# The last layer of a four-layer graph network: a gather per edge tile, or count matrices of block pairs applied by TensorE

## The chip, the cores and the metric

The kernel runs on one core of one Trainium2 chip. The metric is the device time of one execution in microseconds, lower is better. The engines are PE (TensorE, with its weight loads PEld), DVE (VectorE), ACT (ScalarE), POOL (GpSimd, which issues every indirect DMA here) and SP (SyncE, which issues plain DMAs).

## The reference

Four graph layers run one after the other over the same 3,125 nodes of 64 features and the same 103,125 directed edges (src, dst); after each, the result is added to x and normalised over its features. The last one is the one that the change rewrites:

```python
def _L3_gnn_ref(x, edge_index):
    from_, to_ = (edge_index[0], edge_index[1])
    n = x.shape[0]
    deg = jax.ops.segment_sum(jnp.ones_like(to_, dtype=x.dtype), to_, num_segments=n)
    deg_inv = jnp.where(deg > 0, 1.0 / jnp.sqrt(deg), 0.0)
    norm = deg_inv[from_] * deg_inv[to_]
    m_j = norm[:, None] * x[from_]
    out = jax.ops.segment_sum(m_j, to_, num_segments=n)
    return out
edge_index = jnp.stack([src, dst])
...
x = _layernorm(x + _L3_gnn_ref(x, edge_index), axis=-1)
```

Layer L0 is message passing with an edge network (4 inner layers), L1 an attention over edges with a tensor product, L2 message passing with edge features.

## The kernel before, in words

**Orders of the edges.** The nodes are cut into 25 blocks of 128. The edges are sorted twice by block, into 832 tiles of 128 edges each that never cross a block end: order "s" by src for L0, order "d" by dst for L1, L2 and L3. Sorting works in place numbers: DVE and PE compute for each edge its row in the sorted table (`ranks_s_*`, `totals_*`, `places_*`, L406 to L668), and POOL scatters the records there, one indirect DMA for each of 806 columns (`scatter_s_pool` L885, 8 bytes an edge; `scatter_d_pool` L899, 1,136 bytes an edge).

**Records stage.** While POOL scatters order "d", PE and ACT compute the two edge networks of L1 in 202 turns of four columns (`factor_pe` L994, `factor_act` L1030), and DVE copies the other fields of the record (`records_dve` L917). POOL's scatter of turn i waits for ACT's `eo` and DVE's `eo`; both wait until the scatter of turn i-4 has landed. All of it is written out, without loops.

**Messages stage**, four times for L0 and once for L2 (`edge_messages` L1123): 104 turns of 8 tiles. DVE copies 8 index columns (`gi`), POOL gathers 8 tiles of rows (L1161), PE multiplies with one-hot matrices, DVE adds each tile's sum to the block's column of `aggT`, whose number it has loaded into a register (`blocks_of` L1313).

**Attention stage** (`logits_*` L1758 to L1912): 208 turns of four tiles. POOL gathers 4 tiles in each (L1781) and waits for DVE's `gx_read` of four turns before (L1868). Then come the segment maximum by two scans (L1953 to L2060) and the weighted sums (`sums_*`, L2095 to L2155), 104 turns in which DVE adds each tile to its block.

**L3, the part that is rewritten** (from L2330). x times `dinv` is written to `xr` in DRAM; in 104 turns POOL gathers 8 tiles of rows (`conv_pool` L2350), DVE builds the one-hot matrix of the destinations for 8 tiles (L2387) and PE multiplies it with the gathered rows (L2372); DVE adds the 8 products to the blocks of `conv` (L2398), each at an offset from a register:

```python
for t, b in enumerate(blocks_of(dve, "d", i)):
    a = conv[:, bass.ds(b * D, D)]
    ins = dve.tensor_tensor(a, a, bank[j][:, t * D:(t + 1) * D], ALU.add)
```

Loops on an engine are built by `turns` (L105): some turns written out at both ends, the middle as a hardware loop of 2 or 4 turns. `join()` is a barrier of all engines, `meet()` one without POOL. Every engine runs its instructions in program order, and they meet by semaphores.

Of the kernel before, what the change touches and what calls it, by code (L numbers as in the profile page):

```python
# [5 lines left out]
ALU = mybir.AluOpType  # L6
# [59 lines left out]
assert MQ * KQ == TILES["d"] and KQ * H == P  # L66

# [54 lines left out]
def build(nc, x_in, src_in, dst_in, ea16, ea64, ea9, L0_W_in, L0_b_in, L0_eW1, L0_eb1, L0_eW2, L0_eb2, L0_nW1,  # L122
# [3 lines left out]
    with ExitStack() as ctx:  # L126
# [54 lines left out]
        xr2 = dram("xr2", [NPAD, XW])  # L181
        iota_done = sig("iota")
# [75 lines left out]
        bucket8 = tmp("bucket", [P, EC8])  # L258
        bucket = bucket8[:, 0:EC]
        member = tmp("member", [P, EC])  # L260
        onesw8 = tmp("onesw", [P, EC8])
        onesw = onesw8[:, 0:EC]
        rank8 = tmp("rank", [P, EC8])
        rank = rank8[:, 0:EC]
        pos8 = tmp("pos", [P, EC8])
        pos = pos8[:, 0:EC]
        ibuf = tmp("ibuf", [P, EC], I32)
# [17 lines left out]
        keyt = tmp("keyt", [P, 8 * P], BF16)  # L285
        EW = 4
# [664 lines left out]

        whole, left = TILES["s"] // P, TILES["s"] % P
# [41 lines left out]
        def factor_pe():  # L994
# [3 lines left out]
            def turn(k):  # L998
                if k.t == keys_at:
                    keys_pe("s", table_kept)  # L1000
                if k.live(5):
# [87 lines left out]
        for g in range(8, NG):  # L1089
            features_sp(g)  # L1090
        for i in range(records_at, nf):
            records_dve(i)
        for x in namesf:
            sig(x).n += nf
# [28 lines left out]
        def edge_messages(o, local, feature=None, opening={}):  # L1123
# [117 lines left out]
            def messages_dve():  # L1241
                def turn(k):
                    if k.live(0):
# [327 lines left out]
        def scatters_end():  # L1571
            for j in range(AHEAD):
                sp.wait_ge(e_gone[j].sem, e_gone[j].n)
            sp.nop(nofuse=True)
# [64 lines left out]

        weights1_act()  # L1640
# [4 lines left out]
        x_rows_sp()  # L1645
        keys_dve("d", keyt_d)
# [125 lines left out]
        def logits_pool():  # L1772
# [9 lines left out]
            turns(pool, G, depth1, lead1, turn, AHEAD)  # L1782
# [149 lines left out]
        join()  # L1932
# [132 lines left out]
        join()  # L2065
# [17 lines left out]
        join()  # L2083
# [80 lines left out]
        join()  # L2164
# [58 lines left out]
        join()  # L2223
# [37 lines left out]
        conv = sb("conv", [P, NB * D])  # L2261
# [4 lines left out]
        def degrees():  # L2266

            dve.memset(conv[:], 0.0)
# [20 lines left out]
        edge_messages("d", gather_p_features, feature=True, opening={"chunk": degrees})  # L2289
# [44 lines left out]
        cv3 = conv[:].rearrange("p (b f) -> p b f", f=D)  # L2334
        dinv_b = dinv[:].unsqueeze(2).broadcast_to([P, NB, D])
        step(dve.tensor_tensor(sq[:], xn[:], dinv_b, ALU.mult))
        sp.wait_ge(done.sem, done.n)
        sp.nop(nofuse=True)
        loaded.at(sp.dma_start(xr.rearrange("(b p) f -> p b f", p=P), sq[:]), 16)
        sp.wait_ge(loaded.sem, loaded.n)  # L2340
        sp.nop(nofuse=True)
        join()

        n3 = TILES["d"] // W
        names3 = ("gi_set", "oh_set", "summed", "added")
        gi_set, oh_set, summed, added = (sig(x) for x in names3)
        tile_added = sig("part_added")
        rows_in3 = [sig(f"rows_in{j}") for j in range(AHEAD)]

        def conv_pool():  # L2350
            def turn(k):
                if k.live(0):
                    i, j = k.i(0), k.buf(0, AHEAD)
                    pool.wait_ge(gi_set.sem, gi_set.n + i + 1)
                    if k.has(0, AHEAD):
                        pool.wait_ge(summed.sem, summed.n + i - (AHEAD - 1))
                    pool.nop(nofuse=True)
                    for c_ in range(W):
                        pool.indirect_dma_start(gx[j][:, c_, :], None, xr, bass.IndirectOffsetOnAxis(ap=gi[j][:, c_:c_ + 1], axis=0)).then_inc(rows_in3[j].sem, 16)  # L2359
            turns(pool, n3, 4, 6, turn, AHEAD)  # L2360

        def conv_pe():
            def turn(k):
                if k.live(3):
# [3 lines left out]
                    if k.has(3, 2):  # L2368
                        pe.wait_ge(added.sem, added.n + i - 1)
# [39 lines left out]
        for x in names3:  # L2409
            sig(x).n += n3  # L2410
# [40 lines left out]
```

## Time and profile before

| | us |
|---|---|
| median of 3 runs | 14869.3 |
| lowest and highest run | 14853.07, 14883.08 |
| the profiled execution | 14905.94 |
| its span, first to last instruction | 14904.1 |

The profiled execution is 36.6 us above the median of the runs; its span leaves 1.8 us outside. Times in rows are microseconds from the span's start. "[a <-b]" behind a row is how long the engine sat idle before it and what ended that; "issue" means that the profile shows nothing that it waited for.

### The profile page before, as it was taken

How to read it: one execution, taken by the hardware profiler on the slowest of the kernel's cores; microseconds unless marked ns; L12 is line 12 of the kernel's file. 1: busy time of each engine (PE TensorE's matmuls, PEld its weight loads, DVE VectorE, ACT ScalarE, POOL GpSimd, SP SyncE). 2: the span in 40 equal slices, each digit the busy share in tenths (PEclk: the TensorE clock that was granted, in tenths of full speed). 3: DMA queues.
4: the chain of work that ended last, by engine and by line, in shares of the span. 5: the costliest groups of instructions: out<-in, count | busy, mean ns of one | idle time of the engine just before them, and what ended most of it. 6: DMA issues, size and time to landing. Idle time of an engine off the chain costs nothing. (4 is left out here: it accounts for less than half of the span.)

```text
span 14904.1 us, 181222 instructions
## 1 busy us (share of the span) xinstructions
PE 8745.3 (59%) x45043; PEld 7205.7 (48%) x45044; DVE 5993.8 (40%) x14865; ACT 2259.7 (15%) x3991; POOL 7591.8 (51%) x7443
## 2 busy tenths in 40 slices
PE   1003778875656555555556555899994656664333
PEld 0003654443555444445544545788884545554222
DVE  4005740001333333333333333688888833333222
ACT  0000013331000100010001000355551000000000
POOL 4662015555666455646564656355550045554666
PEclk6555557776677667667676776899997767676555
DMA  1001333333111211121111111588883311111111
GB/s 24 1 1 41 108 121 115 114 110 69 40 39 40 60 38 38 39 59 39 39 38 49 39 38 39 166 253 253 253 253 98 97 39 42 41 42 29 22 22 23
DMA packets 853388, 1107.16 MB, mean 74 GB/s; under 512 B 336739, under 2 KB 530568, under 8 KB 852294
## 3 DMA queue, kind: packets, MB, share of 16 engines
q1 hardware_dynamic: 304698, 470.90, 10.8%
q0 software_dynamic: 264160, 418.34, 10.1%
q10 hardware_dynamic: 284332, 215.58, 5.6%
q8 instruction: 87, 1.43, 0.0%
q14 instruction: 111, 0.91, 0.0%
HBM read 896.28 MB, written 207.86 MB: 74 GB/s over the span
## 5 line engine op out<-in xcount | busy, mean ns | idle before, releaser
L1161 POOL DMA_INDIRECT gx_l<-xr,gi_l x4160 | 4269.6, 1026 | 3905.5 <-DVE gi_l L1247 2698.4
L1269 DVE TENSOR_TENSOR aggT_l<-aggT_l,psum 64x128 f32 x4160 | 1160.7, 279 | 3750.8 <-remote 1724.9
L1792 PE MATMUL psum<-cw,xa 128*128 128x256 f32 x6656 | 1509.4, 382 | 22.6 <-DVE xa L1877 20.0
L909 POOL DMA_INDIRECT slots_d<-eo,row_d x806 | 786.4, 976 | 1413.4 <-DVE eo L922 882.1
L1781 POOL DMA_INDIRECT gx<-xr,gi x832 | 920.5, 1106 | 985.6 <-DVEq L1868 629.0
L1792 PEld LDWEIGHTS psum<-cw,xa 128*128 128x128 f32 x6656 | 1232.8, 190 | 237.8 <-issue 85.9
L1323 PE MATMUL psum<-ptab,oht 128*128 x6656 | 1030.8, 309 | 529.2 <-issue 467.5
L1323 PEld LDWEIGHTS psum<-ptab,oht 128*128 128x128 f32 x6656 | 972.0, 225 | 594.1 <-issue 593.2
L1199 PE MATMUL psum<-b,onesb 3*128 3x512 bf16 x520 | 261.0, 502 | 1558.1 <-ACT h_l L1226 1200.6
L2359 POOL DMA_INDIRECT gx_l<-xr,gi_l x832 | 830.5, 998 | 490.7 <-issue 256.7
L1848 ACT COPY xT<-psum 32x512 f32<-32x512 f32 x1664 | 957.4, 575 | 597.7 <-remote 403.7
L895 POOL DMA_INDIRECT slots_s<-rec_s,row_s x806 | 784.1, 973 | 485.5 <-issue 481.0
L1201 PE MATMUL psum<-w,h_l 128*128 128x128 f32 x4160 | 879.6, 377 | 0.0
L1201 PEld LDWEIGHTS psum<-w,h_l 128*128 128x128 f32 x4160 | 748.8, 270 | 181.1 <-issue 181.1
L1199 PEld LDWEIGHTS psum<-b,onesb 3*128 3x128 bf16 x520 | 49.6, 95 | 1624.3 <-issue 1594.5
L1238 ACT ACTIVATE msg_l<-psum 128x512 f32<-128x512 f32 x520 | 310.7, 597 | 3337.1 <-remote 1827.6
L1226 ACT ACTIVATE h_l<-psum 128x512 f32<-128x512 f32 x520 | 310.5, 597 | 3171.3 <-remote 2287.4
L1281 DVE TENSOR_TENSOR pre_s_l<-psum,gx_l 128x512 f32<-128x512 f32 x520 | 359.1, 691 | 1049.2 <-remote 649.5
L1212 PE MATMUL psum<-oh,msg_l 128*64 128x128 f32 x4160 | 740.0, 348 | 64.8 <-issue 64.3
L1212 PE MATMUL psum<-oh_b_l,msg_l 128*64 128x128 f32 x4160 | 687.3, 331 | 52.9 <-issue 47.3
L1212 PEld LDWEIGHTS psum<-oh,msg_l 128*64 128x64 f32 x4160 | 651.9, 183 | 129.2 <-issue 117.4
L567 PE MATMUL psum<-oh_hi,oh_lo 128*128 128x25 bf16 x808 | 37.7, 183 | 1146.1 <-DVE oh_lo L504 883.8
(357 smaller groups left out, 13293.0 us busy)
## 6 DMA issues: line engine op xcount, KB each, us to landing
wkv<-slots_d ACTq DMA_DIRECT2D x208, 568.0 KB
kr<-keyrow_s SPq DMA_DIRECT2D x416, 256.0 KB
shb<-shT SPq DMA_DIRECT2D x1664, 64.0 KB
gx_l<-xr,gi_l POOLq DMA_INDIRECT x4992
vtab<-kv ACTq DMA_DIRECT2D x208, 256.0 KB
v_in<-vtab SPq DMA_DIRECT2D x104, 512.0 KB, 3.5
hT<-noderow SPq DMA_DIRECT2D x101, 512.0 KB
kr<-keyrow_d SPq DMA_DIRECT2D x208, 128.0 KB
```

Source lines behind the costliest of these rows:

```text
L895: scattered[j].at(pool.indirect_dma_start(slots["s"], bass.IndirectOffsetOnAxis(ap=row["s"][:, c:c + 1], axis=0), rec_s[:, c, :], None, bo ...
L909: e_gone[j].at(pool.indirect_dma_start(slots["d"], bass.IndirectOffsetOnAxis(ap=row["d"][:, c0 + t:c0 + t + 1], axis=0), eo[j][:, t, :], N ...
L1161: pool.indirect_dma_start(gx[j][:, c_, :], None, xr, bass.IndirectOffsetOnAxis(ap=gi[j][:, c_:c_ + 1], axis=0)).then_inc(rows_in[j].sem, 16)
L1201: ins = pe.matmul(bank[2][:, q * P:(q + 1) * P], h1[:, q * P:(q + 1) * P], w2[:], start=False, stop=True, skip_group_check=True)
L1212: ins = pe.matmul(sums(j, t // per), msg[j][:, t * D:(t + 1) * D], ohs[j][:, t, :], start=t % per == 0, stop=(t + 1) % per == 0)
L1269: ins = dve.tensor_tensor(a, a, sums(j, h), ALU.add)
L1281: dve.tensor_tensor(pre_s[j][:], bank[0][:, :], gx[r][:, :, :].rearrange("p t f -> p (t f)"), ALU.add).then_inc(pre_done.sem, 1)
L1323: ins = pe.matmul(bank[0][:, t * D:(t + 1) * D], oht[:, t * P:(t + 1) * P], ptab[:, bass.ds(bl[t // PER["s"]] * D, D)], start=True, stop=True)
L1781: pool.indirect_dma_start(gx2[r][:, t, :], None, xr2, bass.IndirectOffsetOnAxis(ap=gi1[j][:, t:t + 1], axis=0)).then_inc(rows_in1[r].sem, 16)
L1792: ins = pe.matmul(bank[2 + p][:, t % 2 * OKV:(t % 2 + 1) * OKV], xa[j][:, c, t * P:(t + 1) * P], cw[:, c, :], start=c == 0, stop=c == KC - 1)
L1848: ins = act.copy(xT2[j][q * DQ:(q + 1) * DQ, h, :], bank[0][h * DQ:(h + 1) * DQ, :])
L2359: pool.indirect_dma_start(gx[j][:, c_, :], None, xr, bass.IndirectOffsetOnAxis(ap=gi[j][:, c_:c_ + 1], axis=0)).then_inc(rows_in3[j].sem, 16)
```

## The change

Every pair (block of src, block of dst) gets its own tiles: a third order of the same edges, with up to 1,432 tiles of 128 slots. A slot holds one number, 128 times the src lane plus the dst lane. L3 then needs no gather: for a tile, a one-hot matrix of src lanes times a one-hot matrix of dst lanes is a 128x128 matrix of counts, and that times the src block of x (held in SBUF as three bf16 parts) is added to the dst block in PSUM.

- **Records stage**: DVE and PE compute the place numbers of the third order between the turns (`pairs_dve(i)` behind `records_dve(i)` for i from 44, `pairs_pe(t)` at the start of a turn of `factor_pe`). SP writes the tiles' block numbers and an empty table at the end.
- **Attention stage**: POOL's part is written out instead of looped, and behind the four gathers of a turn it scatters two columns of the third order (832 in all, 4 bytes a slot). The 416 that are left follow behind the last turn. Barriers from here to L2's messages leave POOL out.
- **L2's messages stage**: SP reads the finished table and the block numbers, DVE splits them into lanes and offsets, once.
- **L3**: 179 turns of 8 tiles, with no POOL in them; PE reads 16 register values a turn.

The core of the diff (plain signals, buffers and the smaller steps of the places left out):

```diff
+TW = TILES["s"]
+PT = (NE + NB * NB * (P - 1)) // P
+PT = -(-PT // W) * W
+NG16 = TW // (2 * W)
+COUNT_AT, RANK_AT = 46, 120
+LAG = 10
+SIDE = 2
...
+        def pairs_dve(i):
...
+            u = i - COUNT_AT
+            if 0 <= u < NG16 // 2:
+                if u >= 4:
+                    dve.wait_ge(pair_counted.sem, u - 3)
+                hot_set.at(dve.tensor_tensor(hot(u, 4), node_iota[:, 0:NB].unsqueeze(1).broadcast_to([P, 4 * W, NB]),
+                                             hi8[:, u * 4 * W:(u + 1) * 4 * W].unsqueeze(2).broadcast_to([P, 4 * W, NB]), ALU.is_equal))
...
+            u = i - RANK_AT - 8
+            if 0 <= u < NG16:
+                dve.wait_ge(pair_ranked.sem, u + 1)
+                step(dve.tensor_tensor(prod.rearrange("p (t b) -> p t b", b=NB), bank[4 + u % 2][:, 0:2 * W * NB].rearrange("p (t b) -> p t b", b=NB),
+                                       hot(u, 2), ALU.mult))
+                pair_picked.at(dve.tensor_reduce(hi8[:, u * 2 * W:(u + 1) * 2 * W], prod.rearrange("p (t b) -> p t b", b=NB), AX.X, ALU.add))
...
+        def pairs_pe(t):
+            u = t - COUNT_AT - LAG
+            if 0 <= u < NG16 // 2:
+                pe.wait_ge(hot_set.sem, u + 1)
+                pe.nop(nofuse=True)
+                for k in range(4 * W):
+                    c = u * 4 * W + k
+                    ins = pe.matmul(spread_ps[:, c:c + 1], hot(u, 4)[:, k, :], ones_b[:], start=True, stop=True, skip_group_check=True)
...
+            u = t - RANK_AT - LAG
+            if 0 <= u < NG16:
...
+                pe.matmul(to, before_b[:], hot(u, 2).rearrange("p t b -> p (t b)"), start=True, stop=True, skip_group_check=True)
+                pair_ranked.at(pe.matmul(to, ones[0:NB, :], diag(u), start=False, stop=True, skip_group_check=True))
...
         for i in range(records_at, nf):
             records_dve(i)
+            pairs_dve(i)
...
+        def pair_scatter_pool(c):
+            j = c // W % 2
+            if c % W == 0 and c >= 2 * W:
+                pool.wait_ge(pair_gone[j].sem, pair_gone[j].n)
+                pool.nop(nofuse=True)
+            pair_gone[j].at(pool.indirect_dma_start(
+                pair_slots, bass.IndirectOffsetOnAxis(ap=pair_row[:, c:c + 1], axis=0), key["s"][:, c:c + 1], None,
+                bounds_check=PT * P - 1, oob_is_err=False), 16)
...
                     for t in range(GT):
                         pool.indirect_dma_start(gx2[r][:, t, :], None, xr2, bass.IndirectOffsetOnAxis(ap=gi1[j][:, t:t + 1], axis=0)).then_inc(rows_in1[r].sem, 16)
-            turns(pool, G, depth1, lead1, turn, AHEAD)
+                    for c in range(SIDE * i, SIDE * (i + 1)):
+                        pair_scatter_pool(c)
+            pool.wait_ge(pair_set.sem, pair_set.n)
+            turns(pool, G, depth1, G + depth1, turn, AHEAD)
+            for c in range(SIDE * G, TW):
+                pair_scatter_pool(c)
...
-        join()
+        meet()
         loop1.close()
...
+        n3, U = PT // W, W // GT
+        depth3, lead3 = 2, 4
+        def conv_dve():
+            def turn(k):
+                if k.live(0):
+                    i, j = k.i(0), k.buf(0)
+                    if k.has(0, 2):
+                        dve.wait_ge(linked.sem, linked.n + (i - 1) * U)
                     dve.tensor_tensor(
+                        from_hot[j][:], node_iota[:].unsqueeze(1).broadcast_to([P, W, P]),
+                        pair_from[:, bass.ds(i * W, W)].unsqueeze(2).broadcast_to([P, W, P]), ALU.is_equal)
+                    dve.tensor_tensor(
+                        to_hot[j][:], node_iota[:].unsqueeze(1).broadcast_to([P, W, P]),
+                        pair_to[:, bass.ds(i * W, W)].unsqueeze(2).broadcast_to([P, W, P]), ALU.is_equal).then_inc(hots_set.sem, 1)
+            turns(dve, n3, depth3, lead3, turn)
+        def conv_pe():
...
+            def turn(k):
+                if k.live(1):
+                    link(k, 0)
+                of, to = blocks(k.i(1)) if k.live(1) or k.live(2) else (None, None)
+                if k.live(2):
+                    apply(k, 2, 1, of[0:GT], to[0:GT])
+                if k.live(1):
+                    link(k, 1)
+                    apply(k, 1, 0, of[GT:W], to[GT:W])
+            turns(pe, n3, depth3, lead3, turn)
```

`link(k, q)` is four bf16 matmuls 128x128x128 into the one bank 7, and waits until ACT has copied the half before out of it; ACT's copy (128x512, to bf16) goes to `links`. `apply` is for each of four tiles a matmul of 128 columns (two parts of x) and one of 64 (the third part), both at offsets of x and of PSUM that come from registers. `blocks` loads 16 register values. The removed loop is the one quoted in the section above.

**POOL at the start of the attention stage.** Before (`gx` are the gathered rows, `gi` their indices):

```order
L1781 DMA gx<-xr,gi 128x320 [waits s_gi1_set]
L1781 DMA gx<-xr,gi 128x320 x3
L1781 DMA gx<-xr,gi 128x320 [waits s_gx_read,s_gi1_set,s_turned1]
L1781 DMA gx<-xr,gi 128x320 x3
L1781 DMA gx<-xr,gi 128x320 [waits s_gx_read,s_gi1_set,s_turned1]
```

and now (L1993 is the same gather, `pair_slots` the third table):

```order
L1993 DMA gx<-xr,gi 128x320 [waits s_gx_read,s_gi1_set,s_turned1]
L1993 DMA gx<-xr,gi 128x320 x3
L1847 DMA pair_slots<-key_s,pair_row 183296x1 [waits s_pair_gone0]
L1847 DMA pair_slots<-key_s,pair_row 183296x1
L1993 DMA gx<-xr,gi 128x320 [waits s_gx_read,s_gi1_set,s_turned1]
L1993 DMA gx<-xr,gi 128x320 x3
L1847 DMA pair_slots<-key_s,pair_row 183296x1 x2
```

Two scatters stand between the gathers of one turn and those of the next; behind the last turn 416 stand in a row, with a wait before every eighth.

**PE in the loop of L3.** Before, a turn is eight matmuls behind one wait:

```order
L2372 MATMUL psum<-gx_l,oh_b_l 128x64 [waits s_added]
L2372 MATMUL psum<-gx_l,oh_b_l 128x64 x7
L2366 REGISTER_ALU
L2369 REGISTER_ALU [waits s_rows_in2,s_oh_set]
L2372 MATMUL psum<-gx_l,oh 128x64 [waits s_added]
```

and now half a turn (ISA rows ahead of a matmul set its offsets):

```order
L2638 MATMUL psum<-to_hot,from_hot 128x128 [waits s_link_kept]
L2638 MATMUL psum<-to_hot,from_hot 128x128 x3
L2625 ISA
L2625 TENSOR_LOAD blk_both
L2648 ISA
L2648 MATMUL psum<-x_parts,links 128x128
L2649 ISA
L2649 MATMUL psum<-x_parts,links 128x64
L2648 ISA
L2648 MATMUL psum<-x_parts,links 128x128
```

The additions to the blocks have gone from DVE into PE's matmuls, and the register values with them.

## Rows read from the trace of the kernel before

**Rows 1.** Busy time by stage: L3, records, attention, scans, sums, and a sorting loop twice.
```profile
core 0: us, PE busy (x) PEld busy (x) DVE busy (x) ACT busy (x) POOL busy (x), PEclk, DMA share, GB/s
13642.00:14883.00 1241.00, 379.32 (x1664) 362.80 (x1664) 317.69 (x1039) 0.00 (x0) 830.49 (x832) 0.50 0.12 22
2143.00:3482.00 1339.00, 1058.73 (x3197) 546.49 (x3195) 63.86 (x255) 434.19 (x599) 786.44 (x806) 0.76 0.34 113
9457.00:11222.00 1765.00, 1728.68 (x9029) 1505.00 (x9030) 1529.75 (x3077) 996.23 (x1859) 920.53 (x832) 0.99 0.85 252
11222.00:11413.00 191.00, 45.54 (x244) 38.71 (x243) 142.48 (x215) 20.54 (x32) 0.00 (x0) 0.62 0.21 35
11413.00:11877.00 464.00, 293.05 (x1664) 270.89 (x1664) 449.95 (x1040) 31.34 (x104) 0.00 (x0) 0.79 0.40 118
190.00:1270.00 1080.00, 19.02 (x408) 15.14 (x408) 76.34 (x102) 0.00 (x0) 748.78 (x771) 0.50 0.02 1
1275.00:1340.00 65.00, 16.92 (x366) 13.53 (x367) 64.68 (x92) 0.00 (x0) 0.00 (x0) 0.50 0.00 0
```

**Rows 2.** Groups of L3's stage, by cost, with what ended the idle time.
```profile
L2359 POOL DMA_INDIRECT gx_l<-xr,gi_l x832 | 830.5, 998 | 490.7 <-issue 256.7 <-DVE gi_l L2382 232.8 <-remote 1.2
L2398 DVE TENSOR_TENSOR conv<-conv,psum 128x64 f32 x832 | 183.5, 221 | 792.5 <-issue 634.9 <-DVE conv L2398 79.7 <-remote 57.7
L740 DVE TENSOR_TENSOR xn<-xn,stat 128x1600 f32<-128x1600 f32 x2 | 3.7, 1826 | 0.1
```

**Rows 3.** Timeline of L3's stage, DVE and POOL, around one of 26 such stretches.
```profile
14202.90 0.22 DVE L2398 TENSOR_TENSOR conv<-conv,psum 128x64 f32 x1 [5.14 <-issue]
14206.42 0.22 DVE L2398 TENSOR_TENSOR conv<-conv,psum 128x64 f32 x1 [3.31 <-issue]
...
14215.12 0.94 POOL L2359 DMA_INDIRECT gx_l<-xr,gi_l  x1 [0.30 <-issue]
...
14220.92 0.22 DVE L2398 TENSOR_TENSOR conv<-conv,psum 128x64 f32 x1 [0.20 <-DVE conv L2398]
14221.33 0.22 DVE L2398 TENSOR_TENSOR conv<-conv,psum 128x64 f32 x1 [0.20 <-DVE conv L2398]
```

**Rows 4.** Timeline of DVE in that sorting loop, beside POOL's scatters.
```profile
614.08 0.37 DVE L502 TENSOR_TENSOR oh_hi<-psum,bucket 128x200 bf16<-128x200 f32 x1 [16.79 <-remote]
...
636.48 0.37 DVE L502 TENSOR_TENSOR oh_hi<-psum,bucket 128x200 bf16<-128x200 f32 x1 [20.90 <-remote]
```

**Rows 5.** The scatter of order "s": POOL's queue and engine, first and last start.
```profile
L895 POOLq MOVE  x806: 2/700/1398, 144.1 to 1272.0; - x162
L895 POOL DMA_INDIRECT slots_s<-rec_s,row_s x806: 969/972/1165, 145.0 to 1269.9; - x162
```

**Rows 6.** Register loads (8 values from `blk_s`, 4 or 8 from `blk_d`) and PE's offset instruction.
```profile
L1316 PEldq TENSOR_LOAD <-blk_s x416: 587/592/4269, 3482.6 to 9328.7; - x139
L1316 PEldq TENSOR_LOAD <-blk_d x312: 331/337/600, 9474.6 to 13575.5; - x156
L1323 PEldq FUSED_REGOPS  x760: 46/46/46, 5017.3 to 6296.5; - x190
```

**Rows 7.** Timeline: bf16 matmuls (8 of 900 columns, 8 of 25), DVE's one-hots back to back.
```profile
1706.01 0.97 PE L619 MATMUL psum<-oh_hi,oh_lo 128*128 128x200 bf16 x8
...
1276.65 0.30 PEld L567 LDWEIGHTS psum<-oh_hi,oh_lo 128*128 128x128 bf16 x8 [8.18 <-issue]
...
1276.72 1.21 DVE L504 TENSOR_TENSOR oh_lo<-psum,pos 128x1024 bf16<-128x1024 f32 x1
1277.85 0.35 DVE L502 TENSOR_TENSOR oh_hi<-psum,bucket 128x200 bf16<-128x200 f32 x1
```

**Rows 8.** Group of the evictions of one PSUM bank in the scans' stage.
```profile
L1977 ACT COPY lrow<-psum 128x512 f32<-128x512 f32 x13 | 6.8, 624 | 8.6 <-PE psum L1971 8.6
```

**Rows 9.** Groups of the records stage; last, ns min/median/max of one.
```profile
L909 POOL DMA_INDIRECT slots_d<-eo,row_d x728 | 710.3, 976 | 491.5 <-issue 245.2 <-ACT eo L1055 237.0 <-DVE eo L922 9.3
L1018 PE MATMUL psum<-einT,kvw 64*128 64x512 f32 x362 | 246.9, 767 | 7.6 <-issue 7.3
L922 DVE COPY eo<-rows_d 128x112 f32<-128x112 f32 x182 | 42.1, 231 | 1148.6 <-DMA slots_d<-eo,row_d 1036.2 <-issue 112.4
...
L1018 PE MATMUL psum<-einT,kvw x398: 589/693/1219, 2145.2 to 3460.0; 64*128 64x512 f32 x199
```

**Rows 10.** The page's groups of the attention stage.
```profile
L1792 PE MATMUL psum<-cw,xa 128*128 128x256 f32 x6656 | 1509.4, 382 | 22.6 <-DVE xa L1877 20.0
L1781 POOL DMA_INDIRECT gx<-xr,gi x832 | 920.5, 1106 | 985.6 <-DVEq L1868 629.0
```

**Rows 11.** POOL's gathers of L2's messages stage, first and last start.
```profile
L1161 POOL DMA_INDIRECT gx_l<-xr,gi_l x824: 940/945/1949, 11999.4 to 13551.1; - x165
```

More of the change, by code:

```diff
@@ L1242, in turn @@
                 def turn(k):
+                    if k.fixed and k.t == 7 and "dve" in opening:
+                        opening["dve"]()
                     if k.live(0):
@@ L2064, in build @@
         ex_set.n += 4
-        join()
+        meet()
         loop3.close()
@@ L2342, in build @@
[L2342 to L2360, printed above, removed]
@@ L2362, in conv_pe @@
-        def conv_pe():
-            def turn(k):
-                if k.live(3):
-                    i, j, b = k.i(3), k.buf(3, AHEAD), k.buf(3)
-                    pe.wait_ge(oh_set.sem, oh_set.n + i + 1)
-                    pe.wait_ge(rows_in3[j].sem, rows_in3[j].n + k.uses(3, AHEAD) * (16 * W))
-                    if k.has(3, 2):
-                        pe.wait_ge(added.sem, added.n + i - 1)
-                    pe.nop(nofuse=True)
-                    for t in range(W):
-                        ins = pe.matmul(bank[b][:, t * D:(t + 1) * D], ohs[b][:, t, :], gx[j][:, t, :], start=True, stop=True)
-                    ins.then_inc(summed.sem, 1)
-            turns(pe, n3, 4, 6, turn, AHEAD)
+        meet()
@@ new lines, in conv_act @@
+        def conv_act():
+            def turn(k):
+                if k.live(1):
+                    i, j = k.i(1), k.buf(1)
+                    for q in range(U):
+                        act.wait_ge(linked.sem, linked.n + i * U + q + 1)
+                        if k.has(1, 2):
+                            act.wait_ge(applied.sem, applied.n + (i - 2) * U + q + 1)
+                        act.copy(links[j][:, q * GT:(q + 1) * GT, :], bank[7][:, :].rearrange("p (t e) -> p t e", e=P)).then_inc(link_kept.sem, 1)
+            turns(act, n3, depth3, lead3, turn)
@@ new lines, in build @@
+        conv_parts_dve()
+        conv_dve()
+        conv_pe()
+        conv_act()
+        hots_set.n += n3
+        cols_set.n += 2 * n3
+        for x in (linked, link_kept, applied):
+            x.n += n3 * U
+        cv_sb = sq[:]
+        dve.wait_ge(applied.sem, applied.n)
+        step(dve.tensor_copy(cv_sb, cv3[:, :, 0, :]))
+        step(dve.tensor_tensor(cv_sb, cv_sb, cv3[:, :, 1, :], ALU.add))
+        step(dve.tensor_tensor(cv_sb, cv_sb, dinv_b, ALU.mult))
+        step(dve.tensor_tensor(xn[:], xn[:], cv_sb, ALU.add))
```

299 lines of the change are left out of this document (245 added, 54 removed).

## The prediction

> **What bounds the kernel now.** I read the stages first, then the groups of L3 by line, then its timeline. The stretch table [rows 1] gives L3 1241 us, in which POOL is busy 830 us, DVE 318 and PE 379, so no engine is full. The groups say why [rows 2]: 832 gathers take 830.5 us, and with 256.7 us of "issue" between them (0.31 each) one costs 1.31 us, 8 in a turn 10.5 us; 104 turns need 1087 us. Another 232.8 us POOL waits for DVE's index copy. DVE is idle most of the time, yet late. The timeline shows its additions 3.5 us apart [rows 3], with nothing that they wait for, as long as POOL issues gather behind gather; once POOL has run dry (last gather at 14215.12) they stand 0.41 us apart. So two things bound L3: POOL's 1.31 us a gather, and a DVE whose instructions come slowly beside an unbroken row of POOL's indirect DMAs.
>
> The same thing happens in the sort. DVE's loop of two instructions a turn made 51 turns in 1080 us beside the scatters of order "s", 21.2 us each, and 46 turns in 65 us without them, 1.41 us each [rows 1]; each turn sits idle 17 to 21 us before its first instruction [rows 4]. In the attention stage, where POOL issues four and then waits for DVE, DVE is busy 1530 of 1765 us, so nothing like it is there. What those stretches have in common is POOL's queue without a wait in it. I take that as the condition; its cause I don't know.
>
> **L3, removed and added.** Removed: 1241 us. Added: 179 turns. Three bounds of a turn:
> - DVE builds two one-hots of 1024 columns. Back to back one takes 1.13 us from start to start [rows 7], so 2.26 a turn, 405 us in all. The rewritten loop has no POOL beside it, and the loop at 1.41 us a turn shows DVE at full pace then.
> - PE streams 8x128 columns for the links and 8x192 to apply them, 2560 in all. 900 bf16 columns in 8 matmuls took 0.97 us at granted clock 0.5 [rows 7], 1.08 ns each: 2.76 us a turn at 1.2 GHz, 1.4 at 2.4 GHz. The weight loads hide (8 with 25 columns each in 0.30 us). A load of 4 register values took 337 ns and one of 8 took 592 [rows 6]; going on by the same step, 16 take about 1.1 us. Sixteen offset instructions of 46 ns are 0.74 us.
> - The chain through bank 7: links 0.55 us, ACT's copy 0.62 us (a mean of 624 ns for 13 copies of that size, [rows 8]) and about 0.1 us for each of two semaphores, twice a turn: 2.8 us.
>
> How they lie: the register load runs while the first four links stream and ACT copies them; then four tiles are applied (0.83 us), the second links stream (0.55), and the other four tiles (0.83) cover most of the second copy. At 1.2 GHz that is 1.2+0.83+0.55+0.83 = 3.4 us, at 2.4 GHz some 3.05. I take 3.3: **590 us**. Lower end 405 (DVE alone), upper end everything in a row, 2.76+1.1+0.74+1.6 = 6.2 us or 1110 us; I stay near the low end because the loads and copies have other engines or older matmuls beside them. Around the loop: four more DVE passes over 1600 elements before it and two behind, 1.8 us each [rows 2], less the write of `xr` and its barrier: +5 us. L3 in sum: -1241+590+5 = **-646 us**.
>
> **Records stage.** DVE gets about 200 us of work (26 one-hots of 800 columns, 52 turns of four operations of 400 columns, 50 passes of 832 or 1432), but is busy 64 us of 1339 [rows 1] and spends 1036 waiting for landed scatters [rows 9]: hidden as long as one turn's part stays under some 5 us, and its largest parts (two passes of 1432) are 3.1 us. PE is the one to look at: 1059 of 1339 us busy. It gets 832 one-column matmuls (0.30 us for 8 as above, 31 us in all), 52 times 400 columns in bf16 (0.43 us) and in f32 (up to 1219 ns for 512 columns [rows 9], so 0.95), 72 us, and some 15 us of sums: 118 us. PE's idle time is 280 us in 202 turns, so between 0 and 118 us shows. I take **+70**, a little over half, since where its clock is low PE has no idle time.
>
> **Attention stage.** PE waits 22.6 us in the whole stage [rows 10] and is the bound at 8.6 us a turn. POOL needs (920.5 + 211)/208 = 5.4 us a turn and waits 985.6 us in all, 629 of them for DVE's `gx_read`. Two scatters at 0.97 busy [rows 5] and 0.31 between are 2.55 us: 8.0 of 8.6. It fits, and the wait in every turn stays. A scatter moves little. I take **+10**; below 0 nothing, since PE loses no work; upper end in the rivals.
>
> **The tail.** 416 scatters stand behind the last turn, 1.28 to 1.40 us each (1126 us for 806, [rows 5]): 532 to 582 us of POOL from 11222 on, until about 11780. The next stage that needs POOL starts at 12000 [rows 11], so nobody waits for POOL itself. But beside it lie the scans (191 us) and about 370 of the 464 us of the sums, whose loop DVE fills to 97% at 4.46 us a turn [rows 1]. If DVE there ran like the sorting loop, 391 us would hold 18 turns, not 88: 311 us lost. If it isn't touched, 0. These scatters wait for their landing in groups of 8 with at most 16 open, those of order "s" in groups of 13 with 26, so the queue is held about half of the time. I take half: **+155**, between 0 and 311, and up to 150 more if the scans suffer (215 instructions at 0.7 us each, the time of POOL's MOVE in [rows 5]).
>
> The Trainium skill ("SBUF — State Buffer", Who interferes with whom) says that only the port pair shared by VectorE and GpSimd makes engines block each other, and that for an instruction's length at a time. By it the tail would cost about nothing; the 21 us a turn above it doesn't explain.
>
> **Small ones.** L2's stage reads and splits the table, ten DVE passes of up to 1432 columns once, +8; two passes before the attention, +2.
>
> Sum: -646 +70 +10 +155 +8 +2 = **-401 us** against the profiled execution, 14906 - 401 = 14505. The median of the runs lies 37 us below that execution; so **14470 us**.
>
> **The rivals.**
> 1. *The tail is free.* For it: DVE's straight-line stretches and the attention loop run well beside POOL, and the scatters have a wait before every eighth. Against: both unbroken rows in the trace slowed DVE. Time: 14470 - 155 = 14315. The skill's rule above would give this one.
> 2. *The tail costs in full*, sums and scans: +156 to +306 on my sum, 14625 to 14775. For it: the sorting loop's row. Against: half the open DMAs.
> 3. *Slower than before: the attention stage becomes POOL's.* Written out, POOL issues two moves and a DMA for each column, and such code went at 0.70 us a MOVE, 1.40 us a column, in the scatter of order "s" [rows 5]. Six columns and three waits would be 10.5 us a turn against 8.6: POOL then has no pause, its row becomes unbroken, and 208 turns cost +400 us, with the full tail (+156) besides. 14470 - 10 + 400 + 156 = 15016. It decides when a POOL turn passes 8.6 us, which is 0.6 us away. Against: the scatter of order "d" is written out too and keeps 0.98 busy with small gaps [rows 9], and POOL slows DVE, which lets it pause again.
> 4. *L3 at 4.5 us a turn* (register load and offsets not hidden): +215, 14685.
>
> **How the numbers follow.** Forecast (half the tail, 14330 to 14600) 0.42; rival 1 0.25; rival 2 0.16; rival 4 0.08; rival 3 0.07; the rest 0.02. The range reaches from rival 1 with L3 at 2.5 us a turn (14315 - 145 = 14170) to the full tail's upper end, 14780; outside lie rival 3 and the mixtures of rivals 2 and 4, and a still faster L3. About 0.2% (30 us) can be told from no change: faster 0.90, same 0.02, slower 0.08.
>
> **What would show it.** L3: from the first one-hot to the last matmul about 600 us, POOL idle there, DVE's one-hots 3.3 us a turn with PE never idle for "issue" beyond the register load. Records: 1339 us to some 1410, with PE busier. Attention: 1765 us, POOL's pause down from 3 to about 0.5 us. Sums: 464 us to about 620, with gaps of 0.7 us or some 20 us before DVE's instructions until POOL's last scatter near 11800, and none after it. I am wrong if the sums keep 464 us, if the attention's turns exceed 8.7 us, or if a turn of L3 is over 4.

## The result and the profile after

The change makes the kernel slower: a median of 15375.8 us over 4 runs (15361.25 to 15383.29) against 14861.2 us before (4 runs), a ratio of 1.034 with a 95% interval of 1.0315 to 1.0364. The forecast was 14470, with a range up to 14780. The profiled execution took 15369.8 us, its span 15367.7; against the span before (14904.1) that is +463.6 us.

The stages of the changed kernel: L3, records, attention up to its last gather, the rest of the attention, scans, sums. Columns as in [rows 1]:

```profile
14556.00:15343.00 787.00, 587.83 (x4296) 415.96 (x4296) 420.20 (x357) 209.45 (x358) 0.00 (x0) 0.50 0.00 0
2142.00:3463.00 1321.00, 1133.90 (x4212) 600.75 (x4210) 284.77 (x594) 431.41 (x600) 820.15 (x806) 0.79 0.34 115
9437.00:11674.00 2237.00, 1878.68 (x9023) 1577.69 (x9024) 1547.42 (x3071) 991.12 (x1852) 1319.84 (x1246) 0.93 0.68 199
11674.00:11989.00 315.00, 55.88 (x131) 34.42 (x129) 25.41 (x47) 10.06 (x20) 218.12 (x223) 0.53 0.06 12
11989.00:12177.00 188.00, 21.16 (x120) 17.21 (x120) 121.02 (x173) 14.63 (x18) 153.26 (x90) 0.55 0.17 19
12177.00:12777.00 600.00, 292.56 (x1664) 270.26 (x1664) 450.59 (x1040) 31.23 (x104) 108.13 (x108) 0.74 0.31 91
```

From these rows and from the first and last instructions of each stage (those of before read the same way):

| stage | before, us | after, us | difference |
|---|---|---|---|
| up to the first gather of the attention | 9457 | 9437 | -20 |
| first to last gather of the attention | 1764 | 2237 | +473 |
| last gather to the end of the attention | 29 | 315 | +286 |
| scans | 163 | 189 | +26 |
| sums | 464 | 600 | +136 |
| update, L2 | 1722 | 1733 | +11 |
| L3's loop | 1243 | 787 | -456 |
| the rest | 62 | 70 | +8 |

L3 does give back 456 us. The four stretches beside which the 832 scatters were to be hidden grow by 921.

The loop of L3 by groups, of the changed kernel (as [rows 2]; 179 turns, 4.4 us each):

```profile
L2648 PE MATMUL psum<-x_parts,links 128*128 x1432 | 368.7, 290 | 148.2 <-issue 148.1
L2609 DVE TENSOR_TENSOR from_hot<-node_iota,pair_from 128x1024 bf16<-128x1024 f32 x178 | 218.0, 1225 | 358.2 <-PE psum L2638 358.2
L2672 ACT CAST links<-psum 128x512 bf16<-128x512 f32 x358 | 209.4, 585 | 589.4 <-PE psum L2638 589.4
```

DVE and ACT both wait for PE; PE waits for "issue". Its timeline over the first half of a turn shows the spacing: 0.29 to 0.34 us from one tile (a pair L2648, L2649) to the next, and a gap of 0.82 us ahead of the first tile, behind which the register load lies. The first tiles of the second half follow one another faster (0.17 us), and then at 0.29 again.

```profile
14901.91 0.58 PE L2638 MATMUL psum<-to_hot,from_hot 128*128 128x128 bf16 x4 [0.46 <-issue]
14903.32 0.28 PE L2648 MATMUL psum<-x_parts,links 128*128 x1 [0.82 <-issue]
14903.48 0.23 PE L2649 MATMUL psum<-x_parts,links 128*128 x1
14903.66 0.28 PE L2648 MATMUL psum<-x_parts,links 128*128 x1
14903.82 0.23 PE L2649 MATMUL psum<-x_parts,links 128*128 x1
14903.95 0.29 PE L2648 MATMUL psum<-x_parts,links 128*128 x1
```

In the attention POOL still waits for DVE, so it is not the bound that rival 3 feared. PE, which had 22.6 us of idle time before its main matmuls [rows 10], now has 305.6, of which 182.0 lie up to the last gather. From the page of the changed kernel:

```profile
L2009 PE MATMUL psum<-cw,xa 128*128 128x256 f32 x6656 | 1631.7, 399 | 305.6 <-issue 224.3
L1993 POOL DMA_INDIRECT gx<-xr,gi x832 | 885.7, 1064 | 915.0 <-DVEq L2085 562.5
```

Behind the last gather POOL has only scatters. There a weight load and its matmul stand 1.40 us apart on PE, or 0.7 in places, and the pair takes 2.80 us, where a matmul took 0.38 us [rows 10] and the weight load was hidden. These steps are two and four times the 0.70 us of POOL's MOVE in [rows 5]; below I call this the pace of 0.70 us. Timeline of the changed kernel:

```profile
11799.66 0.58 PE L2009 MATMUL psum<-cw,xa 128*128 128x256 f32 x1 [1.53 <-issue]
11800.71 0.97 POOL L1847 DMA_INDIRECT pair_slots<-key_s,pair_row  x1 [0.30 <-issue]
11801.05 0.29 PEld L2009 LDWEIGHTS psum<-cw,xa 128*128 128x128 f32 x1 [1.81 <-issue]
11801.99 0.97 POOL L1847 DMA_INDIRECT pair_slots<-key_s,pair_row  x1 [0.30 <-issue]
11802.45 0.58 PE L2009 MATMUL psum<-cw,xa 128*128 128x256 f32 x1 [2.20 <-issue]
...
11805.25 0.58 PE L2009 MATMUL psum<-cw,xa 128*128 128x256 f32 x1 [2.22 <-issue]
```

The last turns of the attention (131 of PE's matmuls were still to come), 29 us before, so become 315. In the sums the same row of scatters lasts until 12323, and up to there they nearly stand still: 80 of 1664 matmuls in 146 us.

```profile
12177.00:12323.00 146.00, 17.89 (x80) 16.95 (x80) 17.94 (x35) 1.36 (x5) 107.14 (x107) 0.56 0.12 33
12323.00:12777.00 454.00, 274.67 (x1584) 253.31 (x1584) 432.65 (x1005) 29.86 (x99) 0.99 (x2) 0.79 0.38 110
```

### The profile page after: what moved, and what is told of

The parts are those of the page before. It is cut to its first block and busy times, and to the rows that moved or that the text cites. A ratio compares the mean times of both kernels' runs of the same rounds, so it can differ in the third digit from the quotient of the medians.

```text
span 15367.7 us, 191464 instructions
## 1 busy us (share of the span) xinstructions
PE 9192.1 (60%) x48687; PEld 7391.4 (48%) x48688; DVE 6367.9 (41%) x14549; ACT 2463.9 (16%) x4349; POOL 7663.9 (50%) x7443
## 5 line engine op out<-in xcount | busy, mean ns | idle before, releaser
L1354 POOL DMA_INDIRECT gx_l<-xr,gi_l x4160 | 4260.2, 1024 | 3720.7 <-DVE gi_l L1442 2514.6
L2009 PE MATMUL psum<-cw,xa 128*128 128x256 f32 x6656 | 1631.7, 399 | 305.6 <-issue 224.3
L2009 PEld LDWEIGHTS psum<-cw,xa 128*128 128x128 f32 x6656 | 1307.0, 201 | 569.0 <-issue 391.5
L925 POOL DMA_INDIRECT slots_d<-eo,row_d x806 | 820.7, 1018 | 1373.4 <-DVE eo L938 919.1
L1993 POOL DMA_INDIRECT gx<-xr,gi x832 | 885.7, 1064 | 915.0 <-DVEq L2085 562.5
L1847 POOL DMA_INDIRECT pair_slots<-key_s,pair_row x832 | 913.7, 1098 | 297.0 <-issue 288.8
```

Source lines behind the costliest of these rows:

```text
L925: e_gone[j].at(pool.indirect_dma_start(slots["d"], bass.IndirectOffsetOnAxis(ap=row["d"][:, c0 + t:c0 + t + 1], axis=0), eo[j][:, t, :], N ...
L1847: pair_gone[j].at(pool.indirect_dma_start(pair_slots, bass.IndirectOffsetOnAxis(ap=pair_row[:, c:c + 1], axis=0), key["s"][:, c:c + 1], No ...
L1993: pool.indirect_dma_start(gx2[r][:, t, :], None, xr2, bass.IndirectOffsetOnAxis(ap=gi1[j][:, t:t + 1], axis=0)).then_inc(rows_in1[r].sem, 16)
L2009: ins = pe.matmul(bank[2 + p][:, t % 2 * OKV:(t % 2 + 1) * OKV], xa[j][:, c, t * P:(t + 1) * P], cw[:, c, :], start=c == 0, stop=c == KC - 1)
```

## The experiments

One thing first, since several numbers can't be read without it. The runs came in groups (e1 to e4, e5 to e8, e9 to e11, f1 to f4, g1 to g3), and beside them the kernel before took 14591 to 14861 us in some and 11472 or 11489 us in others. I call the first the slow pace and the second the fast pace, for reasons that come out at the end. Ratios are to the kernel before in the same group. Stage times are also set beside those of other groups at the slow pace; the gathers of the attention take 1764 us in the kernel before at 14861 us and 1761 at 14591 (g2), so this stage hardly moves between them.

**Which of the scatters cost what.** Four kernels beside one another, at the slow pace (kernel before: 14627 us). `e1` leaves out the tail:

```diff
-            for c in range(SIDE * G, TW):
-                pair_scatter_pool(c)
```

> Leaves out the last 416 of the 832 scatters of the third order (the table then lacks half the edges); the two per turn of the attention stay. The changed kernel spent 315 us from its last gather to the end of the attention (before: 29), 188 us in the scans (164) and 600 us in the sums (464). If the tail does that: these go back to about 30, 164 and 464, the time falls by about 446 us to 14925, and the 204 turns before it stay at 10.9 us. Rival (the attention's turns are late because PE lags for another reason, and the tail is innocent): the last turns still take 300 us and the time stays near 15370.

`e2` also leaves out the scatters in the turns (first piece below), `e3` makes POOL's part a loop again on top of that (second), and `e4` is `e1` with one scatter a turn (third):

```diff
-                    for c in range(SIDE * i, SIDE * (i + 1)):
-                        pair_scatter_pool(c)
...
-            turns(pool, G, depth1, G + depth1, turn, AHEAD)
+            turns(pool, G, depth1, lead1, turn, AHEAD)
...
-SIDE = 2
+SIDE = 1
```

> Leaves out all 832 scatters (the table stays empty); POOL's part of the attention is still written out. If the scatters do the harm, a turn of the attention is back at 8.6 us and the stage at about 1790 us: 14925 - 474 = 14450. Rival (the written-out program of POOL, and not the scatters, slows the others): the turn stays near 10.9 us and the time near 14925.

> As e2_none, and POOL's part of the attention is a hardware loop again. Scatter theory: the same as e2_none within 20 us, 14450. Rival of the written-out program: this one alone comes to 14450, with e2_none near 14925.

> One scatter per turn instead of two, and none behind the attention (208 of 832 in all; the table lacks the rest). Theory A (a threshold: POOL needs a pause in each turn, and two scatters leave it too short, 2.1 to 3.7 us of waiting where one would leave some 3): a turn stays at 8.6 to 8.7 us, the time is at most 40 us above e2_none, about 14450 to 14490. Theory B (each scatter has its price, whatever the pause: 474 us for 416 is 1.14 us each): 208 of them cost 237 us, about 14690.

Ratios: e1 0.9993 (0.9973 to 1.0014), e2 0.974 (0.970 to 0.978), e3 0.975 (0.971 to 0.978), e4 0.982 (0.978 to 0.986). Without the tail the last turns, scans and sums are back at 29, 163 and 466 us: the tail costs what the table above says, 448 us (in e7 and e8 below, which keep the tail, the last turns take 315 and 313 us again). Written out or looped, the gathers take the same 1760 us, so the written-out program is innocent. And without any scatter the change is 2.6% faster even at the slow pace: L3's gain is real, and the scatters eat it. The attention's gathers take 1760 us with none, 1899 with one and 2166 with two scatters a turn. The windows of e2, e4 and e1, one kernel a row, columns as above:

```profile
9273.00:11032.00 1759.00, 1728.67 (x9025) 1504.80 (x9026) 1529.74 (x3076) 994.69 (x1856) 900.35 (x832) 0.99 0.86 253
```
```profile
9263.00:11162.00 1899.00, 1753.33 (x9026) 1497.66 (x9027) 1532.14 (x3075) 993.76 (x1857) 1112.52 (x1039) 0.99 0.80 235
```
```profile
9329.00:11495.00 2166.00, 1831.18 (x9028) 1544.01 (x9028) 1548.72 (x3076) 994.03 (x1858) 1355.03 (x1246) 0.96 0.70 206
```

Both theories on e4 miss: the first scatter of a turn costs 0.67 us, the second 1.28. Not even one is free, and there is no fixed price. In all three DVE is busy about as long; PE's idle time grows (before its main matmuls from 16.1 us in e2 to 210.6 in e1, 111.6 of it for DVE's `xa`), and its clock falls with it (0.99 to 0.96).

**Is it POOL's time, or the DMA?** In the next group, again at the slow pace (kernel before 14811 us):

```diff
-                        pair_scatter_pool(c)
+                        idle_s.at(pool.memset(idle_t[:], 0.0))
+                        pool.wait_ge(idle_s.sem, idle_s.n)
```

> In place of the two scatters of each turn of the attention POOL runs two memsets of 128x1024 of about 1 us each, behind one another; no scatter anywhere (the table stays empty). The first run of this study with two scatters per turn and no tail had 2166 us from the first to the last gather of the attention (10.4 us a turn), with one 1899, with none 1760 (8.46). Theory P (POOL's time is what counts, it comes late to its gathers): about 2100 to 2200. Theory D (it is what an indirect DMA does beside the others): 1760 to 1800.

The gathers take 1782 us. Windows of the attention and POOL's group (9400 to 11300) of this kernel:

```profile
9361.00:11143.00 1782.00, 1734.44 (x9026) 1503.90 (x9027) 1579.74 (x3076) 994.85 (x1856) 1298.89 (x1246) 0.99 0.84 250
```
```profile
L1996 POOL MEMSET idle_t<- 128x1024 f32 x407 | 391.2, 961 | 11.8
```

Memsets as long as the scatters (961 ns against 1.0 us; only the 0.30 us between two DMAs is missing) cost 22 us over the 1760 without any (ratio 0.9735, 0.9694 to 0.9775), where with two scatters a turn the gathers of this group take 2222 and 2234 us (e7 and e8, below, which keep them). So it is not POOL's time that counts: what hurts is something that an indirect DMA does, or that its issue does. Whether that is the write, `e6` was to say, with a bound that drops all slots but those of row 0:

```diff
-                bounds_check=PT * P - 1, oob_is_err=False), 16)
+                bounds_check=0, oob_is_err=False), 16)
```

> The scatters of the attention stay, two per turn, but the bound is row 0, so that nearly every slot is dropped and hardly a packet is written; the last 416 are left out (the table stays empty). Theory W (the 4-byte writes load the DMA queues and HBM, and hold up other transfers): the attention's gathers take 1760 to 1800 us. Theory I (what counts is the DMA instruction on POOL, whatever it writes): about 2166, as with the writes.

The gathers take 2221 us, as long as with the writes, so dropping the writes helps nothing (ratio 1.0044, 1.0015 to 1.0074). But the page counts the same 250848 packets and 391.27 MB in the software queue as for e1, so as many packets were handled all the same. The values written don't matter; packets and instruction stay unseparated.

**What sets the turn of L3.** Same group as e5. `e7` takes the registers away, `e8` a matmul:

```diff
-                both = nc.values_load_multi_w_load_instructions(
...
-                return both[0::2], both[1::2]
+                at = [t * 3 * 2 * D for t in range(W)]
+                return at, at[::-1]
```

> L3 with fixed block numbers in place of the 16 register values of a turn: no register load, no offset instructions; the same matmuls go to wrong blocks. All scatters stay. Theory S (PE's own instruction stream sets the turn of 4.4 us: 1.1 us of load and 0.30 us a tile): the turn falls to 2.8 to 3.0 us, L3's loop from 787 us to 500 to 540. Theory C (the round trip through the one link bank and ACT's copy sets it): the turn stays over 4 us, the loop over 716 us.

```diff
-                    pe.matmul(PS[:, bass.ds(to[t], 2 * D)], of_tile_, x_flat[:, bass.ds(of[t], 2 * D)], start=False, stop=True, skip_group_check=True)
-                    ins = pe.matmul(PS[:, D:][:, bass.ds(to[t], D)], of_tile_, x_flat[:, NB * 2 * D:][:, bass.ds(of[t], D)],
-                                    start=False, stop=True, skip_group_check=True)
+                    ins = pe.matmul(PS[:, bass.ds(to[t], 2 * D)], of_tile_, x_flat[:, bass.ds(of[t], 2 * D)], start=False, stop=True, skip_group_check=True)
```

> L3 applies two bf16 parts of x and leaves the third out: one matmul of 128 columns per tile instead of 128 + 64. All else as changed. Theory S (PE's instruction stream): a tile costs 0.15 us less, a turn 1.2 us less, the loop 787 to about 570 us. Theory C (streamed columns at 1.2 GHz): 8x64 columns are 0.43 us a turn, the loop about 710 us.

The loop takes 441 us in e7 (2.46 us a turn) and 623 in e8 (3.48 a turn); the ratios are 1.009 (1.008 to 1.011) and 1.021 (1.018 to 1.024). L3's windows of e7 and of e8:

```profile
14418.00:14859.00 441.00, 260.81 (x4296) 217.79 (x4295) 419.85 (x357) 209.43 (x358) 0.00 (x0) 0.99 0.00 0
```
```profile
14497.00:15120.00 623.00, 401.31 (x2864) 275.08 (x2863) 419.76 (x356) 209.46 (x358) 0.00 (x0) 0.50 0.00 0
```

Theory S holds: PE's instruction stream is the bound. Without register load and offsets DVE's two one-hots fill the loop (420 of 441 us), and PE is granted 0.99 of its clock (the level of 2.4 GHz) where it had 0.50 (1.2 GHz) with the offsets in its line. That clock has a part in e7's gain, which no run separates. e8 stays at 0.50: one matmul less per tile is worth 0.92 us a turn there, less than the 1.2 expected and more than its 512 columns, which at the prediction's 1.08 ns each are 0.55.

**Rows with pauses, and the scatters elsewhere.** `e9` keeps all 832 scatters and gives the tail a full wait ahead of every fourth; `e10` has none in the attention, 416 behind it with such waits, and 416 in L2; `e11` is e10 with two parts. The first piece is of e9, the second, for L2, of e10:

```diff
-            if c % W == 0 and c >= 2 * W:
+            if c >= SIDE * G:
+                j = 0
+                if c % 4 == 0:
+                    for g_ in pair_gone:
+                        pool.wait_ge(g_.sem, g_.n)
...
+                        if "pool" in opening:
+                            opening["pool"](i)
```

> The changed kernel, all 832 scatters in their places, but the 416 behind the attention stand in groups of four, and before each group POOL waits until all earlier ones have landed (instead of eight, with sixteen open). Theory R (an unbroken row of POOL's indirect DMAs is what slows the loops of the others; a pause frees them): the attention ends about 30 us after the last gather (315 as changed), scans 164, sums 464 to 500, the tail takes 104 x (5.2 + 2) = 750 us and fills the time up to L2; the time falls by 350 to 440 us against the changed kernel, to a ratio of about 1.005 to 1.01 to the kernel before. Theory N (what counts is the number of such DMAs, 1.07 us each as measured, wherever the pauses are): the stretch to L2's first gather stays as long, ratio about 1.03.

> No scatter in the attention; 416 behind it in groups of four with full waits; the other 416 in L2's messages, four behind the eight gathers of each turn, with the same waits; the table is read and split behind L2 (about 15 us). Computes everything. Theory R: attention 1790 us, scans 164, sums up to 500; POOL waits 462 us in L2 now and gets 545 us of work and some 200 us of landing waits there, so L2 grows by 100 to 350 us. Sum with L3 at 787: ratio 0.985 to 1.0. Theory N (each scatter costs 1 us anywhere): 832 us over the kernel without scatters (0.974), ratio about 1.03.

> As e10_moved, and L3 applies two bf16 parts of x and leaves out the third. L3's loop took 623 us with that instead of 787. If the two add: 164 us under e10_moved, ratio 0.974 to 0.989 by theory R, the version that beats the kernel before; by theory N about 1.02.

These runs fell in the fast pace: the kernel before takes 11472 us. Ratios 0.9966 (0.9956 to 0.9975), 1.0415 and 1.0274. In e9 the attention's gathers take 1771 us with their two scatters a turn, as good as none. So these runs say nothing on theory R under the conditions of the result. They do rule out the placement in L2: its stage grows from 1078 us (e9) to 1604, since POOL's turn there is now twelve DMAs in a row, 15.3 us; it waits only 21.7 us for landings in the whole stage, so the waits are not what makes it long. Two parts take off 163 us here too (e11). So I ran the changed kernel itself, e9 again, and both with two parts:

> The changed kernel itself, as the measure for the three beside it. On a chip on which the kernel before takes 14600 to 14900 us: ratio 1.034 as before. On a chip like that of the last three runs (kernel before 11472 us, no instruction at a pace of 0.7 us): if the slow pace is the cause of the loss, the two scatters a turn cost nothing (1771 us for the attention's gathers, measured in e9), the tail ends before L2 and costs nothing either, and the ratio is 0.98 to 0.99; if the loss has another cause, it stays over 1.

> e9_tail_in_fours again. On a chip of the slow pace, theory R (unbroken rows; pauses free the others): last turns 30 us, scans 164, sums 464 to 500, the tail some 750 us long; 350 to 440 us under f1. Theory N (number of DMAs): within 60 us of f1. On the other kind of chip: about 150 us over f1, since the tail ends later than L2 wants POOL.

> f2 with two bf16 parts of x in L3 (the third left out), 164 us less in L3 as in e8. On a chip of the slow pace by theory R ratio 0.993 to 1.0 with the attention's loss of 400 us still in it; by theory N about 1.02. On the other kind 0.982.

> f1 with two parts in L3, the kernel of e8. 164 us under f1 on either kind of chip: ratio 1.022 at the slow pace, about 0.97 on the other kind.

Again the fast pace (kernel before 11489 us). Ratios: f1 **0.9821** (0.9805 to 0.9838), f2 0.9961 (0.9947 to 0.9976), f3 0.9823, f4 **0.9677** (0.9661 to 0.9693). The very change that is 3.4% slower above is 1.8% faster here. Its stages (f1: attention from 5 us behind its first gather, scans, sums, L3):

```profile
6805.00:8569.00 1764.00, 1729.25 (x9029) 1508.40 (x9030) 1559.81 (x3077) 994.48 (x1858) 1383.87 (x1242) 1.00 0.87 252
8597.00:8761.00 164.00, 20.77 (x120) 17.36 (x120) 120.96 (x174) 14.28 (x19) 134.27 (x70) 0.55 0.19 22
8761.00:9229.00 468.00, 286.71 (x1664) 264.19 (x1664) 450.61 (x1041) 31.37 (x104) 365.99 (x315) 0.80 0.42 117
10464.00:11251.00 787.00, 588.18 (x4296) 415.15 (x4296) 420.18 (x357) 209.44 (x358) 0.00 (x0) 0.50 0.00 0
```

With the same scatters in the same places, attention (1769 us from the first to the last gather), scans and sums take within 10 us of what they take without any; L3, in which POOL does nothing, takes 787 us at both paces. How much of the 1.8% is L3's gain isn't known, since no trace of the kernel before was taken at the fast pace. The last three runs fell in the slow pace again (kernel before 14591 us):

> The tail's scatters in groups of four with full waits, once more. Where the kernel before takes 14.6 to 14.9 ms: theory R (pauses free the loops) ratio 1.005 to 1.01, theory N (number of scatters) 1.03. Where it takes 11.5 ms: 0.996 as twice before.

> The kernel before itself, for its profile on this chip. Where it takes 11.5 ms: L3 is bound by POOL's gathers at 1.25 to 1.31 us each, 1040 to 1090 us instead of 1241, with DVE's additions no longer 3.5 us apart, so that L3 is worth 250 to 300 us to the change there (787 us new) and not 452. Where it takes 14.6 to 14.9 ms: stages as in the profile of the kernel before.

> All 832 scatters left out (the table stays empty). Where the kernel before takes 11.5 ms the scatters cost nothing that shows: 5 to 30 us under the changed kernel, ratio 0.979 to 0.982. If they had a price of their own there too (0.3 us each, say), it would be 250 us, ratio 0.96. Where it takes 14.6 to 14.9 ms: 0.974 as before.

g1 has a ratio of 1.0109 (1.0076 to 1.0142), g3 0.973 (0.9705 to 0.976), g2 0.9992 as it should; L3's loop is 1212 us in g2. The stretches of g1 from the first gather on, cut as in the table above:

```profile
9236.00:11374.00 2138.00, 1812.07 (x9021) 1527.66 (x9022) 1550.26 (x3074) 991.08 (x1852) 1361.37 (x1246) 0.97 0.71 208
11374.00:11407.00 33.00, 26.60 (x132) 22.17 (x131) 24.02 (x45) 9.91 (x20) 18.58 (x19) 1.00 0.40 108
11407.00:11570.00 163.00, 21.59 (x120) 18.20 (x120) 120.43 (x173) 14.30 (x19) 110.99 (x49) 0.55 0.18 22
11570.00:12036.00 466.00, 291.57 (x1664) 269.40 (x1664) 450.61 (x1041) 31.36 (x104) 225.87 (x210) 0.79 0.41 117
```

Theory R holds for the tail: the same 416 scatters, with a pause for landing after every fourth, take nothing from the last turns (33 us for 315), the scans (163 for 188) or the sums (466 for 600). POOL's MOVE ahead of a scatter is 29 ns throughout g1, where the changed kernel has up to 1415. The tail itself then lasts until 12290, 916 us where 750 were expected, and L2 starts at 12298 instead of about 12150; that is what is left of its cost. In the attention the two scatters a turn still cost 378 us (2138 against 1760 in g3), although POOL does pause there.

## Why the prediction was wrong

- **L3, -646: measured -456.** The mechanism was right, one term was too small, the time of PE's line. The register load came out as estimated (1106 ns by the profile, 1.1 estimated). What failed is the price of four applied tiles, 0.83 us "streamed at 1.2 GHz": the offset instructions and the matmuls' issue stand in one line on PE, 0.31 us a tile in the timeline above, 1.2 us for four, and the load too stands in that line. Measured are 4.4 us a turn, nearly rival 4's figure (priced 4.5), to which I gave 0.08. I had priced the offsets at 0.74 us and then let older matmuls cover them; in the trace nothing does. e7 shows it: without loads and offsets, 2.46 us, with the higher clock as part of that.
- **Records, +70: measured 0** (1327 us before, 1321 after, first to last scatter). PE's extra 75 us of busy time (1133.9 against 1058.7, in a window 18 us shorter) all went into idle time.
- **Attention, +10: measured +473, and this is the step that turned the sign.** The prediction read the stage's bound correctly (PE, 8.6 us a turn; POOL's 8.0 fits) and concluded from "nothing like it is there" that a queue with a wait in every turn harms nobody. It was a yes-or-no reading of one point, four DMAs a turn. e4 and e1 show a rising curve: 0, 0.67 and 1.95 us a turn for none, one and two. Rival 3, the one on the slower side, had the place right, and its +400 us came near the +473 by luck, for its mechanism was wrong: its POOL has no pause, but POOL waits 562 us for DVE in the profile, and a POOL kept nearly as busy by memsets costs 22 us (e5).
- **Tail, +155 at half: measured +448.** The bounds (0 to 311, and 150 for the scans) were taken from scans and sums; scans +26 and sums +136 together are inside them. What is outside is a piece that I left out: the turns that are in flight behind POOL's last gather, 29 us of work that became 315. They lay in the window that I called the scans [rows 1], but I priced that by DVE's 215 instructions and not by PE's 244 matmuls. The condition, a row without a pause, was right (g1); that "half the open DMAs" would be half as bad was not. The sums lost nearly half of 311 us only by luck: they stood almost still, but for 146 us instead of some 370, since the slowed last turns had used up the rest of the tail.
- **Rival 1, the tail is free.** The Trainium skill ("SBUF — State Buffer", Who interferes with whom) allows DVE and POOL to block each other only over their shared port. At the slow pace the trace shows a slowing that this rule doesn't cover: PE, which by that section shares nothing with POOL, needs 2.80 us for a weight load and its matmul. At the fast pace the tail was indeed free (f1: 28, 164, 468 us).
- **The range** was drawn from one execution's stages as if the pace of 0.70 us were always there. It isn't: the runs at the fast pace don't have it.

**What a better version does.** Two parts of x instead of three (f4, which leaves the third bf16 part out) and the tail as changed are 3.2% faster than the kernel before at the fast pace, and 1.5% faster than the changed kernel; at the slow pace the same kernel (e8) stands at 1.021. No version that was run with all 832 scatters beats the kernel before at the slow pace; the nearest is g1 at 1.011. g1 with two parts would, by an estimate from e8's 164 us in L3, come to about 1.00; this wasn't run at that pace.

## What to carry to other kernels

An engine that is idle is not free to use: price what is put on it by what its instructions do to the others, and look for that at more than one dose before you call a place safe. When register offsets feed small matmuls, count the instructions in the engine's line before the columns (here up to 0.31 us a tile, and 1.1 us to load 16 values). And where a move hides work behind a stage's last item, look at what is still in flight at that moment, not only at the stages that follow.

## What the runs showed of the hardware that I had not expected

The same program takes 14.6 to 14.9 ms in some groups of runs and 11.5 ms in others. The difference doesn't lie in L3 without POOL (787 us in both), nor in the attention with four gathers a turn (1759 to 1764 us in both; e10 for the fast pace), but where POOL issues longer rows of indirect DMAs: the last scatter of the records stage ends at 3463 us in the changed kernel of the result and at 2283 in f1. POOL's own MOVE between two scatters shows it, first in the changed kernel of the result, then in f1 for the third order and for order "s" (ns, minimum/median/maximum):

```profile
L1847 POOLq MOVE  x832: 3/29/1415, 9438.6 to 12324.1; - x167
```
```profile
L1847 POOLq MOVE  x832: 29/29/29, 6801.4 to 9233.6; - x167
L911 POOLq MOVE  x806: 29/29/39, 142.7 to 1184.2; - x162
```

In the kernel before at the slow pace, the MOVE of that scatter has a median of 700 ns and a maximum of 1398 [rows 5]; in f1 it never takes more than 39. Likewise DVE's sorting loop: 51 turns in 1080 us [rows 1] beside the scatters there, while f1 runs through all 202 turns of both sorting loops by 1030 us, beside the same scatters:

```profile
L518 DVE TENSOR_TENSOR oh_hi<-psum,bucket x202: 336/351/367, 157.3 to 1030.3; 128x200 bf16<-128x200 f32 x101
```

So the pace of 0.70 us beside an unbroken row of indirect DMAs doesn't belong to the program: the same one runs with it and without it, and the durations of single instructions stay nearly the same (this one-hot of DVE 351 ns in f1, 365 in the changed kernel at the slow pace). Nor is it shown to belong to a chip. The record gives the chip of e5 to e8 (slow) and that of e9 to e11 (fast, 17 minutes later) the same number, 9; whether they are one chip at two times or two chips of different machines isn't recorded. What makes the pace stays open. A row of scatters with a wait for landing after every fourth doesn't bring it on (g1).

That the attention's loss is the same effect isn't shown either. It too is absent in f1, and other work on POOL doesn't cause it (e5), but POOL's MOVE ahead of a scatter is 29 ns throughout e1 and e4, and the trace of the changed kernel has PE's steps of 0.7 us in the attention only in places, here in a stretch of POOL's six DMAs of a turn:

```profile
10508.33 0.19 PEld L2009 LDWEIGHTS psum<-cw,xa 128*128 128x128 f32 x1 [0.76 <-issue]
10508.91 1.00 POOL L1847 DMA_INDIRECT pair_slots<-key_s,pair_row  x1 [0.30 <-issue]
10509.04 0.38 PE L2009 MATMUL psum<-cw,xa 128*128 128x256 f32 x1 [1.07 <-issue]
10509.76 0.19 PEld L2009 LDWEIGHTS psum<-cw,xa 128*128 128x128 f32 x1 [1.24 <-issue]
10509.77 0.47 PE L2009 MATMUL psum<-cw,xa 128*128 128x256 f32 x1 [0.36 <-issue]
10510.22 1.00 POOL L1847 DMA_INDIRECT pair_slots<-key_s,pair_row  x1 [0.30 <-issue]
10510.48 0.19 PEld L2009 LDWEIGHTS psum<-cw,xa 128*128 128x128 f32 x1 [0.54 <-issue]
```

Beside rows of four PE is hardly held up (g1's tail, e2's attention), beside rows of five it is, and beside those of six and more clearly (e4, e1); a wait between a turn's gathers and its scatters would test whether the length of the row decides, and wasn't run. A change that trades POOL's DMAs for work elsewhere, or adds some, can have opposite signs at the two paces, as this one has: 1.034 and 0.982.
